# The copy of the transposed attention output moves from VectorE to ScalarE

## The reference

```python
t = t + _L3_attn_ref(_ln_t(t), Wq, Wkv, Wo, bo)          # 8 images, 256 tokens, 128 channels

def _L3_attn_ref(hidden_states, Wq, Wkv, Wo, bo):
    HEADS, DIM_HEAD = 8, 16
    q = hidden_states @ Wq
    k, v = jnp.split(hidden_states @ Wkv, 2, axis=-1)
    # q, k, v are split into 8 heads of 16
    scores = jnp.einsum('bqhd,bkhd->bhqk', q * scale, k).astype(jnp.bfloat16)
    probs = jax.nn.softmax(scores, axis=-1)
    out = jnp.einsum('bhqk,bkhd->bqhd', probs.astype(jnp.float32), v)
    out = out.astype(jnp.bfloat16)
    return out.reshape(B, S, H * dh).astype(jnp.float32) @ Wo + bo
```

## Time and profile before

| what | value |
|---|---|
| median of 3 runs | 593.65 us (593.54 to 595.31) |
| the profiled execution's own time | 596.83 us |
| its span | 595.0 us |
| PE busy in the span | 462.4 us (78%) |
| DVE busy | 411.5 us (69%) |
| ACT busy | 256.8 us (43%) |
| mean granted clock of PE | 0.874 |

### The profile page before, as it was taken

How to read it: one execution, slowest core, us unless ns; L and a number is a source line. 1 busy time by engine, 2 the same in 40 slices (tenths; PEclk the granted TensorE clock), 3 DMA queues, 4 the chain that set the end, 5 groups by cost and what they waited for, 6 DMA issues and landing times. The chain is left out here.

```text
span 595.0 us, 10094 instructions
## 1 busy us (share of the span) xinstructions
PE 462.4 (78%) x3070; PEld 368.5 (62%) x3070; DVE 411.5 (69%) x1117; ACT 256.8 (43%) x538; POOL 290.1 (49%) x274
## 2 busy tenths in 40 slices
PE   8898883879668999999617878888657897777652
PEld 4685672859543899999516867777547364556431
DVE  4728659998877448644358589999896965555534
ACT  3722233300310774444234688788822043333324
POOL 3094448879434777777314021111120177777750
PEclk9998787998657999999957799999955799998995
DMA  6000070000360111112140010000005012122226
GB/s 236 1 1 2 0 283 0 1 1 1 132 221 13 50 51 54 50 53 52 53 120 10 11 26 18 18 20 24 12 0 143 0 50 55 49 52 53 52 58 195
DMA packets 29388, 33.03 MB, mean 56 GB/s; under 512 B 4065, under 2 KB 24418, under 8 KB 29218
## 3 DMA queue, kind: packets, MB, share of 16 engines
q1 hardware_dynamic: 24354, 22.26, 11.8%
q0 software_dynamic: 4992, 10.23, 6.6%
HBM read 20.16 MB, written 10.36 MB: 51 GB/s over the span
## 5 line engine op out<-in xcount | busy, mean ns | idle before, releaser
L1112 POOL DMA_INDIRECT xg<-rows_in,idx x78 | 76.3, 978 | 36.7 <-issue 21.3
L1118 POOL DMA_INDIRECT rows_out<-yo,idy x78 | 76.8, 985 | 30.5 <-issue 18.4
L1481 DVE TENSOR_TENSOR hidden<-ps,hidden 128x512 fp32r<-128x512 f32 (+1 forms) x78 | 43.3, 556 | 42.2 <-ACT hidden L1177 42.2
L1170 ACT ACTIVATE hraw<-ps 128x512 f32<-128x512 f32 (+1 forms) x78 | 38.3, 491 | 79.3 <-PE ps L1278 79.3
L1299 PE MATMUL ps<-wHL,hidden 128*128 x234 | 69.6, 349 | 0.6 <-DVE hidden L1481 0.4
L1302 PE MATMUL ps<-wHL,hidden 128*128 x234 | 54.3, 232 | 0.0
L1489 DVE TENSOR_REDUCE yo<-ps 128x128 f32<-128x256 f32 x78 | 32.7, 419 | 24.9 <-PE ps L1302 16.6
L1163 ACT ACTIVATE xa<-ps 128x128 fp32r<-128x128 f32 x78 | 21.8, 280 | 62.8 <-PE ps L1264 62.8
L1299 PEld LDWEIGHTS ps<-wHL,hidden 128*128 128x128 f32 x234 | 44.6, 191 | 3.5 <-issue 1.6
L1302 PEld LDWEIGHTS ps<-wHL,hidden 128*128 128x128 f32 x234 | 45.1, 193 | 0.0
L1622 POOL CAST vp<-v3f 128x256 bf16<-128x256 f32 x8 | 3.5, 436 | 80.4 <-ACT s L1653 80.4
(11 more groups left out here) (299 smaller groups left out, 1274.8 us busy)
## 6 DMA issues: line engine op xcount, KB each, us to landing
wraw<-in_ex SPq DMA_DIRECT2D x2, 2048.0 KB, 9.9
rows_in<-both SPq DMA_DIRECT2D x8, 512.0 KB, 6.3
both<-rows_out SPq DMA_DIRECT2D x16, 256.0 KB, 4.1
wraw<-in_ex SPq DMA_DIRECT2D x1, 3072.0 KB, 11.0
k3M<-k3S SPq DMA_DIRECT2D x60, 32.0 KB, 1.8
w<-in_pack SPq DMA_DIRECT2D x1, 1582.0 KB, 9.7
xg<-rows_in,idx POOLq DMA_INDIRECT x78, 2.6
rows_out<-yo,idy POOLq DMA_INDIRECT x78, 2.3
```

The source lines that it names most:

```text
L1112: pool.indirect_dma_start(xg[:, j % NXG, :], None, xs_d[:], bass.IndirectOffsetOnAxis(idx[:, j:j + 1], 0)).then_inc(ld[j % NXG], 16)
L1118: pool.indirect_dma_start(ys_d[:], bass.IndirectOffsetOnAxis(idy[:, j:j + 1], 0), yo[:, j % NYO, :], None).then_inc(st[j % NYO], 16)
L1170: act.activation(hraw[:, j % 2, :], ps[:, HB + j % 2, 0:hid], ACT.Gelu if layer == 0 else ACT.Silu).then_inc(z["act"], 1)
L1481: dve.tensor_tensor(hL[:, j % 2, :], ps[:, HTB + j % 2, 0:hid], hH[:, j % 2, :].bitcast(F32), ALU.subtract).then_inc(z["hL"], 1)
```

## The change

`copy_out` moves from DVE's block to ACT's. It waits for the same two semaphores as before, the transposes of the output (`otp`) and the projection of the image before (`fp`), and raises the same one (`ot`). The operation becomes an ACT copy of the same 128x256 bf16 tile. In a step it stands behind `upper` and before `exponentials`; the copy of the last image stands behind the last `evacuate`.

```diff
@@ block4.scalar
+            def copy_out(b):
+                act.wait_ge(m3["otp"], b + 1)
+                if not isinstance(b, int) or b > 0:
+                    act.wait_ge(m3["fp"], b)
+                act.activation(oT3[:], psb(FB)[:, 0:N], ACT.Copy).then_inc(m3["ot"], 1)
@@ step
                 if there(*fragment(b, g, 5)[:2]):
                     upper(*fragment(b, g, 5))
+                if g == 1 and not first:
+                    copy_out(b - 1)
                 if there(*ahead(b, g, 1)):
                     exponentials(*ahead(b, g, 1))
@@
             images(act, step)
             evacuate(B - 1, 3)
+            copy_out(B - 1)
@@ block4.vector
-            def copy_out(b):
-                dve.wait_ge(m3["otp"], b + 1)
-                if not isinstance(b, int) or b > 0:
-                    dve.wait_ge(m3["fp"], b)
-                dve.tensor_copy(oT3[:], psb(FB)[:, 0:N]).then_inc(m3["ot"], 1)
@@ step
                 if g == 0 and not first:
                     gather(b - 1, 1)
-                if g == 1 and not first:
-                    copy_out(b - 1)
                 if g == 2:
                     gather(b, 0)
@@
             gather(B - 1, 1)
-            copy_out(B - 1)
             pair_apply(dve, 0, c4)
             add(B - 1)
```

## The result

The changed kernel took 598.41 us (median of 5 runs, 597.74 to 600.6), the kernel before 593.65 us in the same comparison; the ratio is 1.0067, with a 95% interval of 1.0044 to 1.0090. It is slower, by 0.4 to 0.7%. Whole executions of one kernel spread: those of before lay between 593.0 and 599.7 us over all comparisons. So I read single effects from the traces, by two numbers that hardly spread: the **loop period** (from the exponentials of one image's step 0 to those of the next, images 3 to 4) and the **stretch** (from the start of image 1's first exponentials to the start of the last addition to `t`, which ends the third attention).

What follows compares the result with a forecast made beforehand. The prediction took a chain between ACT and DVE, 13.25 us an image, as the bound. Its terms, 0.59 + 2.00 + 0.06 + 0.19 + 0.10 = 2.94 us slower, carried 593.65 to 596.6 us; range 593.8 to 598.5 us.

Steps and rivals of the forecast that it cites:

- What bounds the kernel: Third attention: a chain handed between ACT and DVE fills the image's whole 13.25 us period; DVE's copy lies beside it.
- The removed copy is worth nothing: Eight copies leave DVE; in images 1 to 7 the freed 0.20 us only lengthens waits, worth 0 on the chain.
- The wait for PE's transposes: Step 1 on ACT: the copy begins 0.17 us after the exponentials began before, as it needs both output transposes.
- The work: Step 1 on ACT: the copy itself delays the exponentials behind it by 0.33 us, bounds 0.20 and 0.55 us.
- the prediction's own term for image 6: Image 6, written out after the loop: PE reaches the transposes earlier, so the delay is only 0.06 us.
- Image by image: Delays of 0.59 us in image 1, 0.50 each in 2 to 5, 0.06 in 6, 0.19 in 7.
- The last copy: After the steps: ACT's copy is 0.10 us longer than DVE's, and that goes to the end.
- A: Rival: the copy hides in ACT's 0.83 us idle in step 1; only the last copy costs, 593.8 us; chance 0.13.
- B: Rival: DVE's length sets the period, so eight copies give back up to 2.2 us, 591.4 us; chance 0.06.
- C: Rival: the granted clock falls inside the loop, slowing PE, 1.9 us more than the sum, 598.5 us; chance 0.07.
- What the changed profile was to show: Copy on ACT waiting near 1.0 us for PE, exponentials right behind; DVE's `q3H` wait about 0.9 us; loop period 13.75 us.

Runs made afterwards that it cites:

- e2: Changed kernel with the ACT copy moved from step 1 to step 2, behind `q3H` and ahead of the exponentials; 596.38 us, ratio to before 1.0013.
- e4: Kernel before with DVE's copy cut to 8 of its 256 columns, `oT3` zeroed on POOL; 596.74 us, ratio to before 1.0018.
- e8: Changed kernel with ACT's copy cut to 8 of its 256 columns, same place and waits; 596.21 us (1 run), loop period 13.45 us.
- e6: Changed kernel with the ACT copy in step 2 and the second half's division moved from step 0 to step 1; 591.80 us, ratio to before 0.9941.
- e7: Division moved as in e6, but the copy on DVE in step 2 ahead of `q3L`; 593.18 us, ratio to before 0.9962.
- e3: Changed kernel with the ACT copy still in step 1 but behind the exponentials; 596.81 us, ratio to before 1.0020.
- e5: The changed kernel measured again, no edit; 597.84 us, ratio to before 1.0040.
- e9: The kernel of e6 measured again, no edit; 591.25 us, ratio to before 0.9925.

## Why the prediction was right, point by point

**What bounds the kernel** held: the chain between ACT and DVE over `q3H` and the subtractions, not DVE's load. e2 shows it from the one side (copy off DVE and on ACT, off the chain: 96.30 us against 96.25), e4 from the other (copy nearly gone from DVE: no gain).

**The removed copy is worth nothing**: held. In e4 less copy even cost 0.07 us an image, which the prediction did not have.

**The wait for PE's transposes**, 0.17 us: 0.14 us in the trace. From `q3L` of step 0 to the copy it was 393.24 - 389.48 = 3.76 us; to the exponentials before, 392.84 - 389.22 = 3.62 us. PE's values started 2.85 us after `q3L` (392.33 - 389.48), where it was 2.88 before (392.10 - 389.22), which is the difference.

**The work**, 0.33 us: 0.27 us. From the copy to the next copy of scores it is 394.60 - 393.24 = 1.36 us, less the 1.09 us from the exponentials. The neighbour I read it from, `q3H`, had 1.42 us: behind `q3H` the exponentials took 1.07 us and the scores came 1.16 us after their start, behind the copy 1.05 and 1.08. Together 0.41 us an image, and e8 splits it alike. These two terms are what was mis-sized: 0.50 for 0.41. With 0.27 in place of 0.33, the prediction's own term for image 6 is 0.00 us, and -0.01 was measured.

**Image by image**, from the same exponentials in both traces: the interval that holds image 1's copy grew by 0.52 us (predicted 0.59), those of images 2 to 5 by 0.39, 0.41, 0.41 and 0.42 (0.50 each), that of image 6 by -0.01 (0.06), and the rest up to the last addition by 0.21 (0.19 + 0.10). The sum is 2.35 us; I had 2.94.

**The last copy**: PE's projection began 0.44 us after ACT's copy (442.51 to 442.95) and 0.35 us after DVE's, 0.09 us for the 0.10 predicted:

```profile
442.08 0.39 PE L1784 MATMUL ps<-identb,o3b 128*128 128x128 bf16 x2 [1.45 <-DVE o3b L1893]
442.51 0.38 ACT L1673 ACTIVATE oT<-ps 128x256 bf16<-128x256 bf16 x1 [2.45 <-PE ps L1784]
...
442.95 0.39 PE L1790 MATMUL ps<-bo3s,onesb 3*128 3x256 bf16 x1 [0.48 <-ACT oT L1673]
```

**The rivals**: A, hidden, is what e2 makes true by moving the copy one step; in step 1 the transposes alone end after the old start of the exponentials, and the copy's 0.27 us come on top. B, DVE bound, fell in e2 and e4. C fell too: the clock in the loop stayed at 1.00. What the changed profile was to show came as told, but for DVE's wait in step 2, 1.01 us for about 0.9: its subtractions took 0.88 us there (start 394.54), not 1.03 as in the trace of before (start 394.49), where POOL's first piece started during them (395.01) and not behind them (395.69).

**The time**, 596.6 us, is 0.5% over before and lies in both intervals of the measured ratio; the two medians of the changed kernel are 598.4 and 597.8 us, since the 593.65 us that I started from was itself low. That 598.4 us still lies inside the range, just under its upper end of 598.5 us, says little for the mechanism: the first comparison is 4.8 us apart, twice the 2.35 us that the chain lost. What bears the prediction out is the stretch, 2.35 us for 2.94, and the terms above.

## What to carry to other kernels

The engine with the highest busy share need not be the one that sets the period: where it waits in every turn for another engine, follow those waits round until they close, add the legs, and see whether the instruction that is to move lies in a leg or beside one. Here the copy went from a place beside the chain on the busiest engine to a place on the chain of a less busy one, and cost 2.35 us; one step later on the same engine it was free. Time freed beside a chain is worth nothing by itself (e2, e4). What paid was to move work off the chain into a wait beside it, as e6 and e7 did: 2.46 and 2.27 us of the stretch. That DVE's copy had gone to ACT was worth at most 0.19 us of it.

## What the runs showed of the hardware

- An ACT copy of 128x256 bf16 from PSUM to bf16 took 0.37 to 0.40 us (e3, e2), as the fp32 copies of its size do (0.39), and one of 8 columns 0.18 us (e8). In step 1 what follows starts 0.28 us after the start of the long one (the changed kernel) and 0.08 us after that of the short one (e8).
- A DVE instruction was longer with POOL at work beside it: the multiplication into `o3b` took 0.29 us with POOL idle and 0.51 to 0.65 us in the loop while POOL split values (e5, e4). It stands on the chain; with less work on DVE ahead of it the loop came out longer (e4, 13.32 us), by the reading given there.
- The granted clock at the entry of the attention differed between executions of one program (means from 330 to 337 us of 1.00 in e6 and 0.72 in e9, of full speed), and image 0 with it (15.15 and 16.86 us).
